# A shift network and a scan in pieces of 256 columns with an operand in PSUM

## What is computed

```python
h = (x_flat @ W_gat).reshape(M, HEADS, NUM_EXPERTS)
src = jnp.concatenate([edge_index[0], loops])
dst = jnp.concatenate([edge_index[1], loops])
e = leaky_relu(a_src[src] + a_dst[dst])
e_max = segment_max(e, dst); ee = exp(e - e_max[dst])
denom = segment_sum(ee, dst)
msg = h[src] * (ee / denom[dst])[:, :, None]
agg = segment_sum(msg, dst)
```

## Time and profile before

| what | value |
|---|---|
| median of three runs | 8103.55 us |
| the profiled execution: its own time, its span | 8102.29 us, 8100.6 us |
| busy: POOL, DVE, PE, ACT | 4932.5, 3553.2, 3225.1, 1993.6 us |
| the 68 turns of gathers, first start to last end | 2096.1 to 7607.0 us |
| gathers L1153 | 4352, busy 4185.0 us, 1326.2 us of gaps |

### The profile page before, as it was taken

The page is one execution under the profiler, slowest core; times in us unless marked ns, Lnnn a source line. Parts: engine busy times, 40 slices in busy tenths (PEclk is TensorE's granted clock), DMA queues, the critical chain, the costliest instruction groups (busy, mean ns, idle before and its releaser), DMA issues. The chain is left out here.

```text
span 8100.6 us, 53397 instructions
## 1 busy us (share of the span) xinstructions
PE 3225.1 (40%) x14261; PEld 2007.9 (25%) x14323; DVE 3553.2 (44%) x6983; ACT 1993.6 (25%) x3992; POOL 4932.5 (61%) x4847
## 2 busy tenths in 40 slices
PE   7888698998002121212222222212121212221169
PEld 5566575666001010101000010101010101010157
DVE  6888699899532122222222221212122222245367
ACT  6888454554001111111111010111011111111022
POOL 4555200000577777777777777777777777777672
PEclk8999798999556565656566666656565656565579
DMA  3444322221112121212112121212121212111257
GB/s 108 127 129 124 104 91 72 72 83 70 29 31 48 36 49 36 49 36 49 40 45 48 37 49 36 49 36 49 36 49 36 49 36 49 36 48 34 91 187 253
DMA packets 344330, 533.28 MB, mean 66 GB/s; under 512 B 159387, under 2 KB 235978, under 8 KB 319146
## 3 DMA queue, kind: packets, MB, share of 16 engines
q1 hardware_dynamic: 196210, 471.31, 16.7%
q0 software_dynamic: 147904, 59.58, 7.2%
HBM read 299.94 MB, written 230.45 MB: 65 GB/s over the span
## 5 line engine op out<-in xcount | busy, mean ns | idle before, releaser
L1153 POOL DMA_INDIRECT e_got<-rows,e_index x4352 | 4185.0, 962 | 1326.2 <-issue 1326.2
L1606 PE MATMUL ex_y_ps<-ex_hh,w_w 128*128 128x512 f32 x1024 | 630.6, 748 | 3791.0 <-ACT ex_hh L1624 3784.3
L1224 DVE TENSOR_TENSOR e_adv<-e_got,e_near 128x256 f32<-128x256 f32 x68 | 53.6, 789 | 3037.6 <-DMA e_got<-rows,e_index 2962.7
L1606 PEld LDWEIGHTS ex_y_ps<-ex_hh,w_w 128*128 128x128 f32 x1024 | 237.4, 242 | 4146.1 <-ACT ex_hh L1624 3837.3
L1168 ACT ACTIVATE e_index<-p_both 128x64 int32 (+1 forms) x68 | 17.3, 256 | 3888.0 <-DMA e_got<-rows,e_index 3888.0
L1588 PE MATMUL ex_hid_ps<-ex_tn,w_w 128*128 128x512 f32 x1024 | 597.4, 714 | 225.0 <-DMA ex_tn<-norm 225.0
L506 PEld LDWEIGHTS o_y_ps<-w_w,o_hh 128*128 128x128 f32 x4096 | 536.6, 192 | 257.9 <-issue 236.6
L669 POOL DMA_DIRECT2D keys<-s_upper x1 | 0.6, 587 | 957.9 <-DVEq L792 957.9
L506 PE MATMUL o_y_ps<-w_w,o_hh 128*128 128x128 f32 x4096 | 541.5, 275 | 16.8 <-ACT o_hh L526 16.8
L492 PE MATMUL o_hid_ps<-o_tn,w_w 128*128 128x512 f32 x1024 | 525.9, 596 | 3.3 <-DMA o_tn<-norm 3.3
L1641 DVE SCALAR_TENSOR_TENSOR ex_z<-ex_y_ps,w_b,ex_gate 128x512 f32<-128x512 f32 x192 | 144.2, 751 | 714.8 <-PE ex_y_ps L1606 714.8
(11 more groups left out here) (375 smaller groups left out, 5907.4 us busy)
## 6 DMA issues: line engine op xcount, KB each, us to landing
e_got<-rows,e_index POOLq DMA_INDIRECT x4352, 2.4
kept<-o_kept SPq DMA_DIRECT2D x64, 1024.0 KB, 4.4
ex_gate<-gate SPq DMA_DIRECT2D x64, 1024.0 KB, 6.6
c_kept<-kept SPq DMA_DIRECT2D x55, 1024.0 KB, 8.2
sums<-e_out SPq DMA_DIRECT2D x68, 768.0 KB, 3.5
m_xin<-in_x_dram SPq DMA_DIRECT2D x64, 512.0 KB, 4.5
mid<-m_xm SPq DMA_DIRECT2D x64, 512.0 KB, 2.9
norm<-m_tn SPq DMA_DIRECT2D x64, 512.0 KB, 4.8
```

Of the source, the lines that this page charges most:

```text
L1153: pool.indirect_dma_start(got[:, at % 2, c, :], None, rows_d, bass.IndirectOffsetOnAxis(ap=index[:, at % 2, c:c+1], axis=0)).then_inc(S["g ...
L1606: last = pe.matmul(self.y_ps[:, :], self.weights.w2[:, e, f, :], self.hh[:, e % 2 * HID + f, :], start=(f == 0), stop=(f == HID - 1))
```

## The change

The 13 bits of the network are spread over nine turns: two bits each in turns 2 to 5, one each in turns 62 to 66, and they now run as `Ends.shift` at the end of DVE's body, behind the chunk and the tile. Each step is cut into pieces of 256 columns. `bit` stays in SBUF, now 256 columns wide, and `moved` becomes 256 columns of float32 in PSUM: the unused half of `beside`'s bank, which is now allocated in full (`spare`). The scan of turn 1 and what stands around it (`gap`, the product) is cut into 17 pieces of 256 columns as well, with `gap` in the same place in PSUM. `gap` moves from turn 0 into turn 1, and a copy of the last column carries the scan from piece to piece.

```diff
-    BLOCKS, GROUP, FIRST = WIDTH // P, 7, CHUNKS - 4
-    BITS = (range(0, 5), range(5, 9), range(9, SHIFT_BITS))
+    BLOCKS, GROUP, PIECE = WIDTH // P, 7, 256
+    BITS = {2: range(0, 2), 3: range(2, 4), 4: range(4, 6), 5: range(6, 8), 62: (8,), 63: (9,), 64: (10,), 65: (11,), 66: (12,)}
...
+        self.moved, self.gap = spare, spare
...
-        self.bit, self.moved = flow[:, 0:WIDTH], flow[:, WIDTH:2*WIDTH]
-        self.gap = self.bit[:, 0:RUN].bitcast(BF16); self.lag = self.moved[:, 0:RUN]
+        self.lag, self.bit = flow[:, 0:RUN], flow[:, RUN:RUN+self.PIECE]
...
-        return k < 2 or k >= self.FIRST
+        return k < 2 or k >= CHUNKS - 1
...
-            go(v.tensor_scalar(self.gap, kept.start[:, :], -1.0, 1.0, ALU.mult, ALU.add)); settle()
...
-            go(v.tensor_tensor_scan(self.lag, self.gap, self.gap, self.lead[:, :], ALU.add, ALU.max)); settle()
-            go(v.tensor_tensor(word[:, P:WIDTH], self.lag, kept.start[:, :], ALU.mult)); settle()
...
+            before = self.lead[:, :]
+            for i, a in enumerate(range(0, RUN, self.PIECE)):
+                cols, held = slice(a, min(a + self.PIECE, RUN)), self.carried[:, i%2:i%2+1]
+                gap = self.gap[:, 0:cols.stop-a]
+                go(v.tensor_scalar(gap, kept.start[:, cols], -1.0, 1.0, ALU.mult, ALU.add)); settle()
+                go(v.tensor_tensor_scan(self.lag[:, cols], gap, kept.start[:, cols], before, ALU.add, ALU.max)); settle()
+                go(v.scalar_tensor_tensor(out=word[:, P+a:P+cols.stop], in0=gap, scalar=0.0, in1=self.lag[:, cols], op0=ALU.is_equal, op1=ALU.mult))
+                go(v.tensor_copy(held, self.lag[:, cols.stop-1:cols.stop])); settle()
+                before = held
...
+    def shift(self, v, k):
+
+        word, go = self.word, self.go
+        def settle():
+            v.wait_ge(self.S["dv"], self.n)
+        for b in self.BITS[k]:
+            B = 1 << b
+            for a in range(B, WIDTH, self.PIECE):
+                size = min(self.PIECE, WIDTH - a)
+                far, near, bit, moved = word[:, a:a+size], word[:, a-B:a-B+size], self.bit[:, 0:size], self.moved[:, 0:size]
+                go(v.tensor_scalar(bit, far, b, 1, ALU.logical_shift_right, ALU.bitwise_and)); settle()
+                go(v.tensor_tensor(moved, bit, far, ALU.mult)); settle()
+                go(v.tensor_tensor(far, far, moved, ALU.subtract)); settle()
+                go(v.tensor_tensor(near, near, moved, ALU.add)); settle()
...
-        near = ps("near", [P, 512]); beside = ps("beside", [P, HEADS * COLS])[:, :]
+        near = ps("near", [P, 512]); side = ps("beside", [P, 512]); beside, spare = side[:, 0:HEADS*COLS], side[:, HEADS*COLS:512]
...
-        ends = Ends(nc, during, half, keys, x)
+        ends = Ends(nc, during, half, keys, x, spare)
...
+                    if isinstance(k, int) and k in ends.BITS:
+                        ends.shift(v, k)
```

More of the change, by code:

```diff
@@ L965, with __init__ @@
 class Ends:
-    BLOCKS, GROUP, FIRST = WIDTH // P, 7, CHUNKS - 4
-    BITS = (range(0, 5), range(5, 9), range(9, SHIFT_BITS))
-    def __init__(self, nc, ctx, half, kept, x):
+    BLOCKS, GROUP, PIECE = WIDTH // P, 7, 256
+    BITS = {2: range(0, 2), 3: range(2, 4), 4: range(4, 6), 5: range(6, 8), 62: (8,), 63: (9,), 64: (10,), 65: (11,), 66: (12,)}
+    def __init__(self, nc, ctx, half, kept, x, spare):
         self.kept = kept
+        self.moved, self.gap = spare, spare
         def sb(name, shape, dt=F32): return ctx.enter_context(nc.sbuf_tensor(f"q{half}_{name}", shape, dt))
         self.word = sb("word", [P, WIDTH], I16); flow = sb("flow", [P, 2 * WIDTH], I16)
-        self.bit, self.moved = flow[:, 0:WIDTH], flow[:, WIDTH:2*WIDTH]
-        self.gap = self.bit[:, 0:RUN].bitcast(BF16); self.lag = self.moved[:, 0:RUN]
+        self.lag, self.bit = flow[:, 0:RUN], flow[:, RUN:RUN+self.PIECE]
         span = self.GROUP * P
@@ L999, in __init__ @@
         self.n_of = sb("n_of", [P, 2]); self.ahead_i = sb("ahead_i", [P, 1], I32); self.off_i = sb("off_i", [P, 1], I32); self.block_i = sb("block_i", [P, 1], I32)
-        self.lead = sb("lead", [P, 1]); self.block0 = sb("block0", [P, 1])
+        self.lead = sb("lead", [P, 1]); self.carried = sb("carried", [P, 2]); self.block0 = sb("block0", [P, 1])
         self.pos_ps = (x.y_ps if x else ctx.enter_context(nc.psum_tensor(f"q{half}_pos_ps", [P, 512], F32)))[:, 0:HIS]
@@ L1041, in vector @@
     def vector(self, v, k):
-        S, kept, go, word, bit, moved = self.S, self.kept, self.go, self.word, self.bit, self.moved
+        S, kept, go, word = self.S, self.kept, self.go, self.word
         def settle():
```

## The result

The changed kernel takes **8044.71 us** (median of four runs, 8043.66 to 8052.82); the kernel before, on the same chip, took 8101.23 (four runs, 8098.89 to 8103.63). The ratio is 0.9932, with a 95% interval of 0.9915 to 0.9950: 0.7% faster, 3 us under the forecast of 8048 and inside its range. The profiled execution took 8043.86 us, its span 8042.1.

The account below looks back on a forecast made before the run. The prediction took POOL's 4352 gathers to bound the kernel, DVE costing time only where it holds POOL up. From the 8103.6 us median, -66.0 us of old holds and +10 of new gave 8048 us, range 8034 to 8080.

Parts of the forecast that it names:

- What goes: Gather holds in turns 63 to 65 (54.9 us) and from the scan's part (11.1 us) disappear, together 66.0 us.
- What comes: New holds on gathers from the pieces' products and scalar steps: 10 us taken, 12 us at evenly spread phases.
- A piece: Four DVE steps on 256 network columns: 1.64 us forecast, 202 pieces making 331 us of DVE.
- The cover: Slack between DVE's late chunk 5 and POOL's turn 7: 11.7 us, lasting up to 1.72 us a piece.
- The operand's place decides, not the work: DVE instructions with two SBUF inputs hold gathers; L1240, 2.71 us with one input in PSUM, leaves a gather at 0.94.
- the second rival: POOL falls into step with DVE's pieces, one held gather a piece, 79 to 101 us; 8117 to 8139 us; chance 0.09.
- The first: Pieces cost 1.85 to 2.0 us, so POOL's turn 7 waits 19 to 40 us; 8067 to 8088 us; chance 0.11.
- The third: Only scalar steps hold POOL: gain 17 us less some 6 for short ones, about 8093 us; chance 0.03.

Follow-up runs that it names:

- the SBUF scan: Against the changed kernel: network's pieces with `moved` as int16 in SBUF, and the scan's `gap` as float32 in SBUF too; 8044.21 us, ratio 0.9929.
- the int16 kernel: Against the changed kernel: `moved` as int16 in SBUF, 256-column pieces, the scan's `gap` still in PSUM; 8038.62 us, ratio 0.9920; repeated, 8038.41 us.

## Why the prediction was right, and where its reason was not

**What goes: right.** 54.9 us from turns 63 to 65: in the changed kernel they are 1.5 us above no hold at all. 11.1 us from the scan's part: the holds of turns 0 and 1 fell by 10.9 (POOL's two turns 14.7 before, 3.8 after), and the old form put back costs 10.6.

**What comes: mis-sized.** I took 10 us of new hold. The sum of all holds, 17.9, is 7.2 above what was left of the old 76.7 without the 66.0. Of it 5.2 end some 0.81 us behind a product, nothing measurable comes from the scalar step, and most of the rest is the gates' instructions, which met the gathers in another phase and held them for 5.6 us in place of 4.2; that I had not counted. I had reckoned 12 us for product and scalar step at evenly spread phases, over twice too many. The phases are not spread: with four gathers to three pieces, a gather is held for 0.08 us once in four, and it is the gather that holds the scalar step (last section). With 7.2 in place of 10 the sum is 8045 us; the median is 8044.71. That 10 came so near is in part luck, as one term was too high and another left out.

**A piece: right.** 1.66 us for 1.64. The scalar step is 0.269 for 0.227 (see the last section), the steps with a PSUM input 0.412 for 0.422. The Trainium skill has a dearer PSUM source ("VectorE: DVE Perf Modes", section "The TRN2 errata"), by which each such step would be an estimated 0.065 us longer. That does not show: 0.412 us with a float32 input in PSUM stands beside 0.417 with one in SBUF. The working also charged it to three steps, though the product's inputs lie in SBUF; for the two with a PSUM source the Trainium skill's figure there would give an estimated 1.77 us a piece in place of 1.84, and some 7 us on the sum in place of 17.

**The cover: the mechanism right, an input left out.** Chunk 5 ended 40.0 us later than before (2647.4 for 2607.4), where I said 52.6. But chunk 1, from which I reckoned, ended 12.0 us earlier than before (at 2292.9, 2304.9), as the scan's holds ahead of it were gone; the lateness gathered from there on is 52.0. I had counted those 11 us for POOL's turn 2 and forgot them for DVE, and POOL's turn 7 itself came 6.8 us earlier (2664.88). So the cover was 11.7 + 12.6 - 6.8 = 17.5 us. That the cover is real, and what it costs when spent, the kernels with 128 columns and with the old turns show.

**The step that failed: "The operand's place decides, not the work".** That sentence explained L1240 against L1073 rightly, but for the network it put the gain down to PSUM. The runs put it down to the cut: with short steps and no PSUM operand in the network, about 46 of its 55 us are gone (float32 in SBUF, 9 left) or practically all (int16 in SBUF), and the int16 form in SBUF is the faster one (int16 in PSUM was not run). Among the kernels in pieces the place decides only for the scan, whose piece of 0.75 us is long enough to lock POOL. At full width no kernel here has the network's operand in PSUM, so what the place alone would give there stays open.

**Why the cut works.** In the kernel before, a step of two inputs takes 2.49 us for a full width, and a gather that starts inside waits for the rest of it; a bit cost 54.9 / 13 = 4.2 us of hold, for up to 1.32 + 3 x 2.49 + 0.14 = 8.9 us of DVE. Of the network's hold 36.7 us end some 0.8 us behind a two-input step, and 17.1 us 0.11 us behind a scalar step. A step of 0.29 to 0.43 us leaves a window of only some 0.2 to 0.3 us in which a gather's start is held. What is left depends on the beat between piece and gather. By the second rival's arithmetic (lockstep of one gather a piece where the window, the instruction less about 0.12 us, is longer than the piece less 1.25): 0.31 against 0.41 in the changed kernel and 0.30 against 0.43 with float32 in SBUF, no such lockstep, and none of one to one is seen; 0.63 against 0.41 under the SBUF scan, and 0.22 against 0.16 with 352 columns, lockstep, seen in both; 0.17 against 0 with int16 and 256 columns, where falling into step costs nothing. The arithmetic fits five kernels as far as one to one goes; it was not put to a test with a window just above and just below its bound. It misses the looser step of four gathers to three pieces, which the changed kernel and the one with float32 in SBUF show (in the latter 49 of 60 cases under a product).

The rows say how that step keeps itself up. The gather at 2330.66 ends at 2331.60 and the scalar step that it holds at 2331.65; the product follows at 2331.68, and the next gather 0.30 us behind the last one's end, at 2331.90: always 0.22 us into the product. So each third piece is set to the gathers again, at a cost to POOL of 0.08 us.

**The rivals.** The first and second were real mechanisms with other sizes than this change has. The third, that only scalar steps hold POOL, is wrong: the 9.66 us gather under a scan, the lockstep under its pieces and the 36.7 us behind two-input steps say otherwise, and under the network's scalar steps, cut to 256 columns, no hold was found. The first half alone of the lock in the Trainium skill ("SBUF — State Buffer", section "SBUF: two separate sides"), instructions in a two-port mode, would have the scan and the two-input steps harmless. Its other half, two SBUF inputs against a GpSimd instruction that reads SBUF, fits these rows if the issue of a gather, whose index lies in SBUF, counts as such; no run here tests that.

## What to carry to other kernels

Where an engine's start-up of a transfer is held up by another engine's long instructions, cut these shorter than the time between two starts and look at the beat between the two periods before giving up a faster data type for another memory. Cutting costs the engine that is cut time, here 307 us of DVE's busy time in the network (85.8 + 83.3 + 83.2 + 54.3) for 99 at full width, so first find where it has slack and how much of a delay the next consumer takes; here cutting and spreading gained only together. And undo a change's parts one at a time even when its time comes out as forecast: the forecast was right to 3 us, with a reason that accounts for some 10 us (4.7 in the network, 5.6 in the scan) of a gain of 58.

## What the runs showed of the hardware

A gather also holds DVE's scalar step. In the changed kernel L1096 usually takes 0.23 us; in 59 of 202 it takes 0.31 to 0.45, mostly 0.36 to 0.39, and these are those that start 0.55 to 0.68 us behind a gather's start: in the timeline above, the step at 2331.28 ends at 2331.65, 0.05 us behind the end of the gather at 2330.66. The mean of 269 ns instead of 227 is this, some 9 us of DVE in all, off the path. In the int16 kernel, where gathers meet the same step of each piece, the mean is 228. I had reckoned with one side alone.

The Trainium skill, "SBUF — State Buffer", section "SBUF: two separate sides", has an exclusive lock that the first comer keeps for its whole instruction while the other blocks. The rows agree in part: each engine holds the other, but 57 scalar steps that start 0.20 to 0.25 us behind a gather's start are not drawn out (the one at 2334.70 above takes 0.23), so the gather does not hold them from its start on.

That two engines fall into step through such holds alone was a rival on paper. The rows of the SBUF scan and of the 352-column pieces show it one to one, those of the changed kernel four to three.
